# Where two expert layers' products land in PSUM, and which half of a projection comes first, in an eight-sublayer fused kernel

## The reference

```
x = x + tanh(g_xattn[l]) * attention_l(layernorm(x), ctx)
x = x + tanh(g_ffn[l])   * ffn_l(layernorm(x))            # l = 0..3
```

## Time and profile before

| | |
|---|---|
| median of 3 runs | 2752.29 us (2749.87 to 2759.57) |
| profiled execution, its own time | 2760.93 us |
| its span, first to last instruction | 2759.1 us |
| TensorE's mean granted clock | 0.960 of full speed |
| PE busy | 2505.1 us, 91% |
| DVE busy | 1815.5 us, 66% |
| ACT busy | 1267.4 us, 46% |
| POOL busy | 1236.7 us, 45% |

### The profile page before, as it was taken

How to read it: one execution, slowest core, us unless ns; L and a number is a source line. 1 busy time by engine, 2 the same in 40 slices (tenths; PEclk the granted TensorE clock), 3 DMA queues, 4 the chain that set the end, 5 groups by cost and what they waited for, 6 DMA issues and landing times.

```text
span 2759.1 us, 42172 instructions
## 1 busy us (share of the span) xinstructions
PE 2505.1 (91%) x13741; PEld 2097.6 (76%) x13741; DVE 1815.5 (66%) x3409; ACT 1267.4 (46%) x3698; POOL 1236.7 (45%) x1379
## 2 busy tenths in 40 slices
PE   4899999998889999999887888888589999999978
PEld 3788888887678888888766776665478888888854
DVE  4777777767677777777756666563377777776652
ACT  2455545454245555555524444223245555555421
POOL 4545544554134444444316556412345444444443
PEclk7999999999999999999999999899889999999979
DMA  3112222222022111111100000259501111110144
GB/s 119 49 47 97 87 96 92 81 100 72 29 77 74 35 39 39 35 33 45 59 8 16 1 1 26 87 183 309 185 23 55 36 36 39 39 32 24 38 177 160
DMA packets 67884, 191.67 MB, mean 69 GB/s; under 512 B 10097, under 2 KB 10737, under 8 KB 64730
## 3 DMA queue, kind: packets, MB, share of 16 engines
q1 hardware_dynamic: 54240, 144.07, 15.9%
q0 software_dynamic: 10224, 42.03, 4.5%
q10 hardware_dynamic: 3210, 2.89, 0.4%
HBM read 170.57 MB, written 52.14 MB: 81 GB/s over the span
## 4 chain that ended last, share of the span: by engine, by line
PE 77%; DVE 7%; issue 4%; POOL 4%; DMA 4%; ACT 3%; ACTq 0%; SPq 0%; POOLq 0%; DVEq 0%
PE B_qkv L733 30%; PE B_out L733 19%; PE B_oT L804 4%; PE B_s L784 4%; PE B_qT L774 3%; PE B_pt L794 3%; PE B_oT L733 3%; PE B_s L785 1%; PE B_oT L871 1%; PE B_s L733 1%; PE B_out L1051 1%; DVE xn L1394 1%; POOL ring_l L2013 1%; DMA qk<-slots_x,tables 1%; PE B_qT L968 1%
## 5 line engine op out<-in xcount | busy, mean ns | idle before, releaser
L1234 ACT ACTIVATE W<-S,nmx 128x128 f32<-128x128 f32 x768 | 297.8, 394 | 45.2 <-DVE nmx L1492 45.2
L2021 POOL TENSOR_SCALAR rn<-ss 128x5 f32<-128x5 f32 x128 | 25.7, 201 | 631.0 <-DVE ss L1435 631.0
L1131 ACT ACTIVATE sq<-B_qkv 128x640 f32<-128x640 f32 x128 | 90.5, 707 | 424.6 <-PE B_qkv L733 424.6
L2042 POOL TENSOR_TENSOR S<-S,mask 128x512 f32<-128x512 f32 x192 | 250.9, 1307 | 20.1 <-ACT S L1072 18.8
L1510 DVE SCALAR_TENSOR_TENSOR X<-B_out,gates,X 128x512 f32<-128x512 f32 x200 | 150.3, 752 | 162.7 <-PE B_out L733 162.5
L2081 POOL TENSOR_TENSOR W<-W,rden 128x512 f32<-128x512 f32 x192 | 200.2, 1043 | 82.4 <-DVE rden L1497 82.4
L733 PE MATMUL B_out<-ring_h,oT_h 128*128 128x512 f32 x516 | 207.1, 401 | 12.3 <-DVE kT L1482 8.3
L733 PE MATMUL B_qkv<-ring_h,xnT_h 128*128 128x512 f32 x512 | 215.2, 420 | 1.4 <-DVE xnT_l L1351 1.4
L784 PE MATMUL B_s<-kT,qT_h 128*128 128x256 f32 x768 | 203.5, 342 | 9.4 <-DVE xnT_l L1351 8.5
L733 PE MATMUL B_out<-ring_h,oT_l 128*128 128x512 f32 x516 | 205.8, 399 | 0.0
L733 PE MATMUL B_out<-ring_l,oT_h 128*128 128x512 f32 x516 | 205.7, 399 | 0.0
(11 more groups left out here) (473 smaller groups left out, 8019.7 us busy)
## 6 DMA issues: line engine op xcount, KB each, us to landing
raw<-in_pieces SPq DMA_DIRECT2D x270, 256.0 KB, 2.6
slots_x<-in_zero SPq DMA_DIRECT2D x32, 1030.0 KB, 6.5
raw<-in_experts SPq DMA_DIRECT2D x16, 768.0 KB, 7.0
w<-in_experts SPq DMA_DIRECT2D x8, 1024.0 KB, 11.9
slots_y<-S SPq DMA_DIRECT2D x31, 256.0 KB, 6.4
sq<-slots_x SPq DMA_DIRECT2D x8, 257.5 KB, 7.2
qk<-slots_x SPq DMA_DIRECT2D x8, 257.5 KB, 7.3
X<-in_x ACTq DMA_DIRECT2D x8, 256.0 KB, 2.9
```

The source lines that it names most:

```text
L1234: t = act.activation(W[:, k, cols(r)], S[:, k, cols(r)], ACT.Exp, bias=nmx[:, k, r:r + 1], accum_out=den[:, k, r:r + 1])
L2042: pool.tensor_tensor(S3, S3, m.unsqueeze(1).to_broadcast([P, R, P]), ALU.add).then_inc(*masked.now((layer, u)))
```

## The change

Three edits. In `project` of the attentions 0, 1 and 3 the 12 key/value matmuls come before the 12 query matmuls; the wait for B_qkv stays in front of both, the waits for the normalised x and the query weights stand between the halves, and the signal `qkv` is given by the last query matmul. ffn0 writes `B_out` in place of `B_oT`. ffn1 writes columns 0 to 511 of `B_qkv` in place of `B_oT`. DVE's additions read the new banks.

```diff
             def project(layer, u):
                 kind, g, b, k, vs = unit(layer, u)
                 five = plan.five[layer, u]
-                pe.wait_ge(*xnT_lo.of((f"attn{layer}", b)))
-                q0, q1 = piece(five[0]), piece(five[1])
-                bank_free("qkv")
-                products(B_qkv[:, 0:HG], [(xn_cols(c, b), two(q0, q1, c)) for c in range(CH)])
                 kv = piece(five[2])
                 for i in plan.ready[plan.ctx[b]]:
                     pe.wait_ge(*piece_lo[plan.items[i]["engine"]].of(i))
+                bank_free("qkv")
                 products(B_qkv[:, HG:HG + 2 * P],
-                         [(ctx_cols(c, b), tuple(m[:, cols(c, 2 * P)] for m in kv)) for c in range(CH)]
-                         ).then_inc(*qkv.now((layer, u)))
+                         [(ctx_cols(c, b), tuple(m[:, cols(c, 2 * P)] for m in kv)) for c in range(CH)])
+                pe.wait_ge(*xnT_lo.of((f"attn{layer}", b)))
+                q0, q1 = piece(five[0]), piece(five[1])
+                products(B_qkv[:, 0:HG], [(xn_cols(c, b), two(q0, q1, c)) for c in range(CH)]).then_inc(*qkv.now((layer, u)))
...
             def ffn0(b):
...
-                bank_free("oT")
+                bank_free("out")
...
-                products(B_oT[:, :], pairs).then_inc(*ffn0_done.now(b))
-                read["oT"] = x_add.of(("ffn0", b))
+                products(B_out[:, :], pairs).then_inc(*ffn0_done.now(b))
+                read["out"] = x_add.of(("ffn0", b))
...
             def ffn1(b):
...
-                bank_free("oT")
-                products(B_oT[:, :], [(xn_cols(c, b), two(w0, w1, c)) for c in range(CH)], [(pick1, bias[:, :])]
+                bank_free("qkv")
+                products(B_qkv[:, 0:D], [(xn_cols(c, b), two(w0, w1, c)) for c in range(CH)], [(pick1, bias[:, :])]
                          ).then_inc(*ffn1_done.now(b))
-                read["oT"] = x_add.of(("ffn1", b))
+                read["qkv"] = x_add.of(("ffn1", b))
```

More of the change, by code:

```diff
@@ L1624, in ffn0 @@
                 dve.wait_ge(*ffn0_done.of(b))
-                add_to_x(b, B_oT, gates[:, 4:5], ("ffn0", b))
+                add_to_x(b, B_out, gates[:, 4:5], ("ffn0", b))
             def fill_pick():
@@ L1634, in ffn1 @@
                 dve.wait_ge(*ffn1_done.of(b))
-                add_to_x(b, B_oT, gates[:, 5:6], ("ffn1", b))
+                add_to_x(b, B_qkv[:, 0:D], gates[:, 5:6], ("ffn1", b))
             def choose2(batch, part):
```

## The result

| | before | after |
|---|---|---|
| median of 4 runs each | 2755.93 us (2749.87 to 2760.11) | 2789.23 us (2781.65 to 2790.78) |
| profiled execution, its own time | 2760.93 us | 2789.0 us |
| its span | 2759.1 us | 2787.2 us |
| TensorE's mean granted clock | 0.960 | 0.954 |

The change makes the kernel slower: ratio 1.0121, 95% interval 1.0102 to 1.014. That is 33.3 us by the medians, where 30.8 were forecast. The forecast time was 2783 us, in a range of 2767 to 2795; of the 6 us between it and 2789.23, 3.6 lie in before's own median, which was 2752.29 us in the runs that the forecast started from and 2755.93 in these. A second set of runs of both kernels in another session gave 2789.09 against 2752.07 us, 1.0128 (1.0107 to 1.0149).

The account below looks back on a forecast made before the run. TensorE was taken to bound the kernel, with 77% of the last-ending chain; ffn0 +30.0, ffn1 -2.0, attention 3 -1.4 and +4.2 gave +30.8 us on a median of 2752.29, forecast 2783 us, range 2767 to 2795.

Parts of the forecast that it names:

- Blocks 3 to 7, the wait: ffn0 blocks 3 to 7: products into B_out wait for the split of the key just transposed there; +28.5 us in sum.
- (c): Rival, ffn0 blocks 3 to 7: the key comes sooner, all five waits like the shortest, 2.9 us; 2767 us; chance 10%.
- The named cause of the late key: ffn0 blocks 3 to 7: ScalarE's key copy stands behind the routing's exponential, before which ScalarE idled 5.14 us in step 70.
- The clock: ffn0 blocks 3 to 7: products run at a lower granted clock after the waits, 31.5 us against 24.7; +6.9 us.
- Blocks 0 to 2: ffn0: old bank waits go, output products may then wait for ffn0's addition; 0, -2.0 and -3.4, together -5.4 us.
- ffn1: Second expert layer: 6.4 us of waits can go, -4.5 remain, new waits of +1.5 and +0.95 for additions; net -2.0 us.
- Unit 0: Attention 3: the key/value half covers the wait of 1.41 us for xnT_lo; -1.4 us.
- Unit 8: Attention 3: query products now come after key/value weights that POOL splits late; 2.9 plus 1.3 for the clock, +4.2 us.
- The seams and the start: Keys and values first: nothing lost at the 192 units' seams (bounds 0 to 0.1 us each) and 0 at the start.
- (d): Rival: the seams cost 0.1 us in each of 192 units, +19 us on top; 2802 us; chance 5%.
- (a): Rival, faster: the bank wait vanishes in ffn0 blocks 3 to 7 too; -15 us, 2737 us; chance 6%.
- (b): Rival, no change: as the faster case, but no clock gain and unit 8 costs 4.2; -7.5 us, 2745 us; chance 5%.

## Why the prediction was right, step by step

**Blocks 3 to 7, the wait: right, and the greater part of the sum.** Five lateness figures from before (4.15, 7.18, 5.86, 8.43, 2.91, sum +28.5) were read as delays. Measured: waits of 31.15 less the old 2.09 and 0.79, +28.3. The rival with shorter waits (c) falls: DVE's chain moved along with PE, and each block's added wait is within 0.3 us of the forecast (4.29, 7.04, 5.60, 8.33, 3.01). Taking the five blocks back shows it; moving the routing and moving ffn0 ahead of turn_q show that the wait is for the key's split.

**The named cause of the late key: wrong in the main.** The prediction said that the split is late because ScalarE's copy of the key stands behind the exponential. In all five blocks that copy had ended 1.7 to 2.4 us before DVE began the split (block 4: 758.46 against 760.38), and block 7 has no exponential between its transpose and its split, yet waits 3.80 us. Between transpose and split the trace shows no idle of DVE longer than 0.36 us: what the key waits for at the end is DVE's own queue of work. Moving the whole routing freed 8.5 us of 31, so the larger part is other work; in block 4 of that run it is DVE's. The size did not depend on this, since it came from the ends of the split.

**The clock: right in size.** Predicted +6.9 for five blocks (its own terms give 31.5 - 24.7 = 6.8). They last 6.15, 6.82, 6.18, 5.84 and 6.38 us, 31.4 together, and 25.0 before: +6.4. Filled waits priced the whole at 8.7, of which before already had part.

**Blocks 0 to 2: the sum close, by luck, from wrong terms.** Predicted 0, -2.0 and -3.4. The two traces must be compared from a common mark: the changed kernel's was already 0.95 us late at unit 60. Less that, block 0's addition on DVE starts at 689.47 (690.42 in the trace), as forecast, and the output products start 0.3 us later than before. But after their wait of 3.15 us they took 4.5 us instead of 3.0, which the prediction did not price, and DVE's chain of block 1, which begins behind them, ended 1.8 us later than the forecast 703.1 (705.83 in the trace). So block 1's output products came at 706.64, 0.4 earlier than before on the common scale and not 2.0. Block 2 gave back more than forecast, 6.1 us and not 3.4: no wait, and its 18 products at a clock of 1.00 instead of 0.59:
```profile
711.60:716.00 4.40, 4.40 (x22) 1.00 0.00 0
```
In all -6.5 in this trace and -3.9 in the second set's, where -5.4 was forecast. The step that failed is that DVE's chain of block 1 ends where it did before: it moved with the clock of PE's products ahead of it.

**ffn1: near in the waits, not shown in the time.** Predicted -2.0. The 6.4 us of waits went; in their place xnT_l grew from 2.3 to 3.3, as forecast, the wait of the output products behind block 1 for kT from 1.33 to 1.96, and 3.2 came for X where 2.45 were forecast. The waits shrink by 1.6 in sum. Alone the edit measures 1.0001; on the trace it cannot be told from nothing.

**Attention 3: both terms short by the clock.** Unit 0: -1.4 predicted for the wait of 1.41. From its first transposes to the next ones PE needs 6.2 us (2008.59 to 2014.82) instead of 9.6 (1984.70 to 1994.33), -3.4: the key/value products run where PE was idle before, and the queries behind them start at distances of 0.23 us instead of 0.43. Kernels without the edit stood at about -1 there, so some 2 are the edit's. Unit 8: +4.2 predicted, +5.3 measured. The wait was right (4.02 in place of 1.24, +2.8 for 2.9); the 24 products behind it ran at half clock for most of their length, 6.8 us instead of 4.5, +2.3 where 1.3 were taken.

**The seams and the start: right.** From unit 132 to unit 186 the gap changes by -0.4 us, so (d), 0.1 us in each of 192 units, falls. The first projection now waits 12.8 us for the context's split, and unit 4 is at most 0.8 us later than before.

**The sum.** By the ledger, about -5 (-3.9 and -6.5), +34.7, 0, -2, +5.3 give +33; the medians give +33.3 and +37.0. The forecast total of 30.8 rests on the five blocks (35.4 forecast, 34.7 and 34.8 in the ledger); the small terms were off by 0.6 to 2 us each and cancel in part, which is luck. Rivals (a) and (b) fall with the five kT waits. Profile against profile the change costs 28.1 us, less than by the medians, since the profiled execution of before was a long one: unchanged stretches differ between executions, the one from unit 186 to the end by -4.4 to +3.0 us from the profile of before.

## What to carry to other kernels

A bank is free for a product when the last reader of its previous content is done, so compare, block by block, the end of that reader with the time at which TensorE arrives, for the old bank and for the new one, and look at who writes that bank next: one name for all blocks gave +33 us, a bank chosen by block (with keys first at unit 0 of attention 3) -18. If the reader's chain hangs on TensorE's own work before it, lateness adds up and can be summed from the rows of before (28.5 us read, 28.3 measured); an edit to that chain is worth something only while TensorE waits for it. Put the half whose operands are surely there first, by unit and not for all: the same swap gained at unit 0 and lost at unit 8.

## What the runs showed of the hardware that was not expected

The same program after the same wait gets a different clock in different executions. Behind block 0 the twelve output products waited 3.14 us in one kernel and 3.15 in another whose instructions up to there are the same; PE alone in the 6 us around them, of the kernel with the five blocks back and of the changed kernel's second set:
```profile
690.00:696.00 6.00, 5.33 (x21) 0.72 0.58 197
```
```profile
689.00:695.00 6.00, 5.44 (x13) 0.50 0.58 203
```
They took 4.3 us (690.67 to 695.00) and 5.5 us (689.56 to 695.02). The output products behind block 1, after waits of 1.67 and 1.66 us, again took 3.0 us in the one and 4.4 in the other. Of the 2.7 us between -6.6 and -3.9 for blocks 0 to 2, the first step makes 1.1 and what follows from the second 1.4. The other traces with these three blocks in B_out, ffn0 at order 66 and the routing in its place fall on the same two values: -6.5 and -6.6 in two (3.0 us for the second group), -3.9 to -4.0 in three (4.4 us). The like happens in ffn1, where the traces of these kernels fall 3 to 5 us apart without an edit that touches it. By a rule of the Trainium skill (TensorE: Matmul & The Clock Gate, "What's actually happening") the number of slow matmuls at the start of a kernel varies from run to run; these two rows show the like in the middle of one.

Filling a wait with products that nobody reads shortened the kernel by 6.7 us although TensorE executed 94 more of them. And the wait of 12.8 us that the new order put at the start cost under 1 us by the ledger (unit 4 stands at +0.8 in one trace of the changed kernel and -0.6 in the other).
